# Flamingo-style block on one Trainium2 core: layer 1 of each chunk routed two chunks behind its controllers, and three tables of expert blocks in place of two

## The chip, the cores and the metric

The kernel runs on one core of a Trainium2 chip. The metric is device time of the whole kernel in microseconds (us), one launch, all data in float32 in device memory at the start and at the end. The engines are named as the profile names them: PE (TensorE, the matrix engine), ACT (ScalarE), DVE (VectorE), POOL (GpSimd) and SP (SyncE, which only issues DMAs).

## The reference

2048 tokens (8 batches of 256) of width 128 pass through two layers. The attention of layer 0 has 16 heads of 8; its feed-forward part is a small mixture of 8 experts that is iterated twice. The attention of layer 1 has one head and no projections, and its feed-forward part is a mixture of 8 experts with 512 hidden units.

```python
x = x + tanh(g_xattn[0]) * cross_attention_16_heads(layernorm(x), ctx)
x = x + tanh(g_ffn[0]) * integrator(layernorm(x))
x = x + tanh(g_xattn[1]) * (softmax(layernorm(x) @ ctx.T) @ ctx)
x = x + tanh(g_ffn[1]) * top2_experts(layernorm(x))

def integrator(xf):                       # E=8 experts, top 2, H=64
    w, idx = top2(softmax(gelu(xf @ rw1 + rb1) @ rw2 + rb2))
    v, s = 0, xf
    for _ in range(2):
        c = concat(s, v)
        # one shared controller and two routed ones, each 256 -> 64 -> 3*128
        for (a, b, g) in controllers(c, idx):
            v_next = sigmoid(a) * v - softplus(b) * (s - mu)
            x_next = s + 0.1 * sigmoid(g) * v_next
        halt = sigmoid(gelu(s @ hw1 + hb1) @ hw2 + hb2)
        s, v = s + halt * (mix(x_next) - s), v + halt * (mix(v_next) - v)
    return xf + iw * (gelu(s @ fw1 + fb1) @ fw2 + fb2)      # "refine"

def top2_experts(t):                      # E=8, FF=512
    pr, idx = top_k(t @ Wr + br, 2); w = softmax(pr)
    return sum(w_e * ((silu(t @ W1[e] + b1[e]) * (t @ W2[e] + b2[e])) @ W3[e] + b3[e]))
```

## The kernel before, in words

The tokens are cut into NC = 4 chunks of CH = 512 (two batches, four tiles of 128 each); L = 3 is the last chunk. Every engine has one stream of instructions, written by hand in program order, and the streams meet at semaphores (`wait_ge`, `then_inc`). No scheduler moves anything: an instruction that waits holds up everything behind it on its engine. PE writes into eight banks of PSUM, and most of the waits in PE's stream say that a bank has been read.

**Layer 0.** Attention of all chunks comes first, then the router of the integrator. The integrator runs with the state transposed (width on the partitions). For a chunk, `hidden_unit` (L1885) makes five groups of hidden units: four for pairs of experts and one for the shared controller and the halt gate. ACT takes their gelu; DVE (`mask_first`, L1292) and POOL (L743 and L749) multiply them by the choice masks of the first and of the second expert. Then PE runs the second matrices of the controllers, `controller` (L1944): one matmul from the shared hidden units (L1947), or one for the biases (L1948) and four for the experts (L1950, which fp32 makes eight in the trace). Three of these parts are for softplus (`soft_part`, k = 0 shared, 1 and 2 routed), up to seven for sigmoids (`gate_parts`, L1997: halt, then three `sig_g`, then, in the second pass, three `sig_a`). Softplus is split: DVE adds the bias and caps at 40 (`capped`, L1308), ACT takes Exp and Ln in place (L910), DVE takes the larger of that and the uncapped value (`uncapped`, L1314). `second_step` (L1380) makes the new state.

The first pass (`it` = 0) goes chunk by chunk. The second (`it` = 1) first makes the hidden units of all four chunks, and then goes chunk by chunk through soft parts and gates. Three PSUM banks (5, 6, 7) take turns for the gates.

**Layer 1, attention.** For a chunk c: `refine_up`, two gelus, `refine_down` (the end of layer 0, L2036 to L2060), `add_refined` on DVE, a layer norm whose rstd POOL makes (`rstd_of_chunk`, L653), `second_columns` (transposes, L2062), `second_scores` for batches 2c and 2c+1 (L2075), their maxima on DVE (`maxima2`), exponentials with sums on ACT (`exps2`), `transpose_probs`, `copy_probsT`, `weigh_context`, and `fuse` on DVE.

**Layer 1, routing.** Third layer norm, `rows_to_columns` (L2119), `route_logits` (L2130), `choose` on DVE (top 2 of 8, L1469), `route_ranks` on PE (L2151; small matmuls that count how many tokens of each expert come before), `weights_of` and `slots_of` on DVE, and `send_rows` on POOL (L769): eight indirect DMAs a chunk write the token rows, sorted by expert, to `sorted_x` in device memory. A slot lies in its expert's region of 2048 slots.

In before, this work of chunks 0 and 1 (in part) fills gaps between the gates of chunks 2 and 3; all that remains of chunks 1, 2 and 3 stands in a list behind the last gate, and then come the blocks.

**Layer 1, experts.** BLOCKS = 39 blocks of 128 sorted rows, each of one expert. SP reads a table that DVE made (which expert, where the rows start) and loads for block j the weights (`load_weights`, L594: 516 KB and 256 KB, four buffers) and the rows (`load_rows`, L604, AHEAD = 3 blocks ahead of the weights). The first EARLY = 9 blocks hold only rows of chunks 0 and 1 (`early_blocks`, L1575) and can start before chunks 2 and 3 are routed; the other 30 come from the second table (`late_blocks`, L1587, made by DVE in block 1). A block is `rows_T` (transpose, L2216), `copy_rowsT` on ACT, `up` (eight matmuls, L2226), four silus (L1056), `gated` on DVE (L1655), `down` (L2237), `keep_result` on DVE (L1647) and `send_result` on POOL (L799). The order on PE is:

```python
rows_T(0); rows_T(1)
for j in range(BLOCKS):
    up(j)
    if j + 2 < BLOCKS: rows_T(j + 2)
    if j: down(j - 1)
down(BLOCKS - 1)
```

Behind the last block the results are read back by token and added to x (the tail).

## Time and profile before

| what | value |
|---|---|
| time, median of 3 runs | 647.35 us |
| lowest and highest | 642.56 and 654.7 us |
| the profiled execution | 639.84 us |
| its span in the profile | 638.0 us |
| granted PE clock, mean of it | 0.945 |
| busy over the span: PE, DVE, ACT, POOL | 87%, 67%, 48%, 32% |

All durations come from the one profiled execution. Its span is the time from the first to the last instruction in the record; the time of the execution is 1.84 us longer. PEld, in the rows, is PE's loading of weights, which runs beside the matmuls. A granted clock of 1.00 is 2.4 GHz. A duration of a group of pipelined matmuls is modelled by the profile, so neighbouring groups overlap a little.

### The profile page before, as it was taken

The page shows a single profiled execution, that of the slowest core. Times are in us where ns is not written, and L with a number is a line of the kernel's source. Part 1 is how long each engine was busy: PE and PEld are TensorE (multiplying, and loading weights), DVE is VectorE, ACT ScalarE, POOL GpSimd, SP SyncE. Part 2 cuts the span into 40 slices and gives each one's busy share as a digit, 9 for nine tenths or more (in the row PEclk, how much of TensorE's full clock was granted, in tenths as well). Part 3 has the DMA queues.
Part 4 walks back from the last instruction along what each step waited for, and adds up shares of the span by engine and source line. Part 5 has one row for each costly group of instructions (what it writes and reads, how often), then busy time and mean ns, then how long its engine had stood idle before and what let it go on. Part 6 is the DMA issues. An engine that isn't in the chain of part 4 may idle for free.

```text
span 638.0 us, 9893 instructions
## 1 busy us (share of the span) xinstructions
PE 555.8 (87%) x3294; PEld 329.1 (52%) x3306; DVE 426.1 (67%) x1055; ACT 307.6 (48%) x630; POOL 203.6 (32%) x214
## 2 busy tenths in 40 slices
PE   3876799999998898999999999998764489999991
PEld 1432344443443343444444454455554488999991
DVE  4898889895387899777335766668756174454455
ACT  2653566666658734554353444455341144444440
POOL 4829301011034360004780500012563622333331
PEclk9895999999999998999999999999986789999997
DMA  8685980000079000000040010000016368999975
GB/s 270 150 193 106 175 166 2 3 2 4 1 256 350 25 1 2 0 0 0 1 131 0 2 18 0 2 0 6 29 35 189 107 201 280 332 325 322 324 246 205
DMA packets 48325, 71.18 MB, mean 112 GB/s; under 512 B 11428, under 2 KB 35428, under 8 KB 47988
## 3 DMA queue, kind: packets, MB, share of 16 engines
q1 hardware_dynamic: 45284, 65.61, 35.5%
q0 software_dynamic: 2272, 4.69, 2.0%
q8 instruction: 26, 0.43, 0.3%
q10 hardware_dynamic: 720, 0.27, 0.2%
q14 instruction: 23, 0.19, 0.1%
HBM read 59.18 MB, written 21.29 MB: 126 GB/s over the span
## 4 chain that ended last, share of the span: by engine, by line
PE 65%; DVE 11%; SPq 6%; DMA 6%; ACT 4%; issue 3%; another core or an unknown queue 2%; POOL 2%; POOLq 0%; DVEq 0%
PE psum L1950 18%; PE psum L2226 9%; PE psum L1895 5%; PE psum L2237 5%; PE psum L1752 4%; PE psum L1765 4%; DMA stacks<-maxT 3%; PE psum L1897 3%; PE psum L1773 2%; PE psum L1947 2%; PE psum L1729 2%; DMA stacked<-parts 1%; SPq L513 1%; PE psum L2086 1%
## 5 line engine op out<-in xcount | busy, mean ns | idle before, releaser
L1950 PE MATMUL psum<-hidden,ew 128*128 128x512 f32 x320 | 145.5, 598 | 1.2 <-ACT halt L927 0.6
L856 ACT ACTIVATE probs<-psum 128x512 f32<-128x512 f32 x128 | 74.6, 598 | 50.1 <-PE psum L1752 49.7
L1950 PEld LDWEIGHTS psum<-hidden,ew 128*128 128x128 f32 x320 | 61.3, 192 | 69.8 <-issue 68.5
L1655 DVE SCALAR_TENSOR_TENSOR gated<-psum,wb,silu_g 128x128 f32<-128x128 f32 x156 | 43.9, 344 | 65.1 <-ACT silu_g L1056 57.8
L1136 DVE TENSOR_REDUCE negmax<-psum 128x4 f32<-128x1024 f32 x64 | 76.8, 1210 | 12.5 <-PE psum L1729 11.9
L2226 PE MATMUL psum<-xbT,wb 128*128 128x128 f32 x624 | 79.9, 283 | 1.6 <-DMA wb<-in_wall_dram 1.3
L1056 ACT ACTIVATE silu_g<-psum,wb 128x128 f32<-128x128 f32 x156 | 44.6, 369 | 70.5 <-PE psum L2226 44.9
L2226 PEld LDWEIGHTS psum<-xbT,wb 128*128 128x128 f32 x624 | 75.9, 199 | 2.6 <-DMA wb<-in_wall_dram 1.7
L799 POOL DMA_INDIRECT sorted_y<-yb,xb x39 | 37.6, 964 | 79.0 <-DVE yb L1647 79.0
L1752 PE MATMUL psum<-stacks 50*128 50x256 bf16 x256 | 49.8, 285 | 8.1 <-DMA stacks<-maxT 5.8
L2237 PE MATMUL psum<-wb,gated 128*128 128x128 f32 x312 | 42.3, 279 | 8.9 <-DVE gated L1655 8.5
L749 POOL TENSOR_TENSOR hidden<-unmasked,chosen 128x512 f32<-128x512 f32 x16 | 24.5, 1536 | 63.3 <-ACT unmasked L906 62.3
L1765 PE MATMUL psum<-probs,v_aug 128*32 128x256 f32 x512 | 44.1, 409 | 0.0
L2237 PEld LDWEIGHTS psum<-wb,gated 128*128 128x128 f32 x312 | 38.7, 195 | 9.3 <-issue 9.3
L779 POOL DMA_INDIRECT sorted_x<-xp,slot x32 | 32.0, 999 | 18.7 <-DVE slot L1519 10.1
L1752 PEld LDWEIGHTS psum<-stacks 50*128 50x128 bf16 x256 | 18.6, 97 | 37.4 <-issue 15.8
L1895 PE MATMUL psum<-xT,ew 128*128 128x512 f32 x64 | 32.8, 600 | 1.3 <-ACT routeT L878 1.3
L656 POOL TENSOR_SCALAR rstd<-meanvar 128x4 f32<-128x4 f32 x16 | 3.8, 239 | 92.5 <-DVE meanvar L1074 92.4
L913 ACT ACTIVATE soft<-soft 128x512 f32<-128x512 f32 x24 | 15.1, 627 | 35.7 <-DVE soft L1311 35.6
L1729 PE MATMUL psum<-stacks 48*128 48x256 bf16 x256 | 29.8, 287 | 0.2 <-DVE negmax L1136 0.2
L743 POOL TENSOR_TENSOR hidden<-hidden,chosen 128x512 f32<-128x512 f32 x16 | 22.2, 1418 | 21.9 <-DVE hidden L1300 21.9
L720 POOL COPY v_aug<-xT 128x128 f32<-128x128 f32 x16 | 4.6, 320 | 71.1 <-PE psum L1765 71.0
(255 smaller groups left out, 962.4 us busy)
## 6 DMA issues: line engine op xcount, KB each, us to landing
wb<-in_wall_dram SPq DMA_DIRECT2D x39, 516.0 KB
wb<-in_wall_dram SPq DMA_DIRECT2D x39, 256.0 KB
sorted_x<-in_slots_dram SPq DMA_DIRECT2D x1, 9815.0 KB, 32.3
stacks<-stacked SPq DMA_DIRECT2D x12, 384.0 KB, 8.2
xb<-sorted_x SPq DMA_DIRECT2D x39, 65.0 KB
stacked<-parts SPq DMA_DIRECT2D x6, 384.0 KB, 3.7
back<-sorted_y SPq DMA_DIRECT2D x4, 512.0 KB, 5.2
stacked<-parts SPq DMA_DIRECT2D x6, 256.0 KB, 3.7
```

The lines of the kernel that those rows point to most:

```text
L799: nc.gpsimd.indirect_dma_start(sorted_y, bass.IndirectOffsetOnAxis(ap=home, axis=0), yb[:, j % X_BUFS, :], None).then_inc(yb_out[j % X_BUF ...
L856: nc.scalar.activation(probs[:, g % 2, h % 4, :, :], s2[n % 2].rearrange("p (k q) -> p k q", k=2), ACT.Exp, scale=float(HD) ** -0.5).then_ ...
L1056: nc.scalar.activation(silu_g[:, j % 2, m, :], bank[j % 2][:, m * P:(m + 1) * P], ACT.Silu, bias=wb[:, j % W_BUFS, B1_AT + m:B1_AT + m + 1 ...
L1136: nc.vector.tensor_reduce(negmax[:, p].rearrange("p h q -> p (h q)"), psum[:, i:i + 2, :].rearrange("p h (q k) -> p (h q) k", q=2), AX.X, ...
L1655: nc.vector.scalar_tensor_tensor(gated[:, j % 2, m, :], bank[2 + j % 2][:, m * P:(m + 1) * P], wb[:, j % W_BUFS, B2_AT + m:B2_AT + m + 1], ...
L1729: last = nc.tensor.matmul(bank[s1[n % 2][h]][:, q * S:(q + 1) * S], qs[64 * h:64 * h + ROWS, p, b * S + q * P:b * S + (q + 1) * P], ks[64 ...
L1752: last = nc.tensor.matmul(s2[n % 2][:, k * S:(k + 1) * S], ks[rows, h // 2, b * S + k * P:b * S + (k + 1) * P], qs[rows, h // 2, b * S:(b ...
L1765: last = nc.tensor.matmul(o[b % 2][32 * j:32 * j + 32, (g // 2) * S:(g // 2 + 1) * S], v_aug[:, b % BC, k, 4 * g + j, :], probs[:, g % 2, ...
L1895: last = nc.tensor.matmul(dst, w[:, 0, :], xT[:, chunk(c)], start=True, stop=not it)
L1950: last = nc.tensor.matmul(dst, ew2[:, j, cols], hidden[:, c, k - 1, j, :], start=False, stop=(j == 3))
L2226: last = nc.tensor.matmul(bank[2 * i + j % 2][:, m * P:(m + 1) * P], w[:, i * FF + m * P:i * FF + (m + 1) * P], xbT[:, j % 2, :], start=Tr ...
L2237: last = nc.tensor.matmul(bank[4 + j % 2][:, 0:D], gated[:, j % 2, m, :], w[:, m * D:(m + 1) * D], start=(m == 0), stop=(m == MT - 1))
```

## The change

**1. Softplus.** `capped` goes from DVE. ACT now reads PSUM itself and takes three functions, Abs, Exp (scale -1) and Ln (bias 1), and DVE adds max(value, 0) in one instruction. The biases of the shared controller and of the halt gate become a 97th row of their matrices, against a row of ones that POOL writes once.

**2. Second pass.** It goes chunk by chunk from the hidden units on. Work of layer 1 stands in fixed places of each chunk's turn: the refine, columns and scores of the chunk before it, and the probabilities, rows, logits and ranks of the chunk two before it. Gates use two banks (5 and 6); routing has bank 7 for itself. The order of gates is sig_g of 1, 2, 0, halt, sig_a of 1, 2, 0. `second_step` has fewer instructions, and `choose`, `weights_of`, `slots_of` of chunk c-2 and the first table stand in it.

**3. Blocks.** The tables are EARLY = 9 (chunks 0 and 1), MIDDLE = 8 (with chunk 2) and LATE = 22. Behind the last gate only the attention of chunk 2 and the refine of chunk 3 are left ahead of block 0; the routing of chunk 2, and scores, fusion and routing of chunk 3, stand between blocks 0 and 12 on all engines. SP waits for a table and its rows before block 9 and before block 17. `rows_T` and `down` have one bank each where they had two. The weights of the second expert are a power on POOL for all chunks (in before chunks 1 to 3 took an exponential on ACT). Context for the second attention is loaded chunk by chunk.

The core of the diff (banks, waits that only follow them, and the layout of `chosen` and of the weights left out):

```diff
@@ softplus on ACT @@
 def softplus(it, c, k):
-    act.wait_ge(capped_ready, 3 * (NC * it + c) + k + 1)
+    n = NC * it + c
+    act.wait_ge(soft_psum, 3 * n + k + 1)
+    if n >= 2:
+        act.wait_ge(state_ready, n - 1)
     t = soft[:, k, c % 2, :]
-    steps.then(nc.scalar.activation(t, t, ACT.Exp))
+    steps.then(nc.scalar.activation(t, soft_bank(it, c, k)[:], ACT.Abs))
+    steps.wait()
+    steps.then(nc.scalar.activation(t, t, ACT.Exp, scale=-1.0))
@@ second pass and the first blocks on PE @@
+for c in range(NC):
+    hidden_units(c)                 # refine_up(c - 1) ahead of its fifth unit
+    soft_part(1, c, 0)
+    if c: refine_down(c - 1)
+    if c >= 2: transpose_probs(2 * c - 4)
+    soft_part(1, c, 1)
+    if c >= 2: transpose_probs(2 * c - 3)
+    soft_part(1, c, 2)
+    if c >= 2: weigh_context(2 * c - 4); weigh_context(2 * c - 3)
+    if c: second_columns(c - 1)
+    gate_part(1, c, 0); gate_part(1, c, 1)
+    if c >= 2: rows_to_columns(c - 2)
+    if c: second_scores(2 * c - 2); second_scores(2 * c - 1)
+    gate_part(1, c, 2); gate_part(1, c, 3)
+    if c >= 2: route_logits(c - 2)
+    gate_part(1, c, 4)
+    if c >= 2: route_ranks(c - 2)
+    gate_part(1, c, 5); gate_part(1, c, 6)
+transpose_probs(4); transpose_probs(5)
+weigh_context(4); weigh_context(5)
+refine_up(L); refine_down(L)
...
 up(j)
 if j + 2 < BLOCKS: rows_T(j + 2)
+if j == 1: second_columns(L)
+if j == 2: second_scores(6)
+if j == 3: route_ranks(2)
+if j == 5: transpose_probs(7)
+if j == 7: rows_to_columns(L)
+if j == 9: route_ranks(L)
 if j: down(j - 1)
+if j == 0: rows_to_columns(2)
+if j == 1: route_logits(2)
+if j == 3: second_scores(7)
+if j == 4: transpose_probs(6)
+if j == 5: weigh_context(6); weigh_context(7)
+if j == 7: route_logits(L)
@@ the same blocks on ACT, behind the silus of block j @@
+if j == 1: copy_xT2(L)
+if j == 5: copy_probsT(7)
+if j == 7: copy_xT3(L)
 if j + 2 < BLOCKS: copy_rowsT(j + 2)
+if j == 0: copy_xT3(2); copy_rows(2)
+if j in (2, 3): exps2(j + 4)        # behind a load of the exp table
+if j == 4: copy_probsT(6)
+if j == 7: copy_rows(L)
@@ the same blocks on DVE @@
+if j == 2: maxima2(6)
+if j == 3: slots_of(2)
+if j == 8: choose(L)
+if j == 9: slots_of(L)
 if j: keep_result(j - 1)
-if j == 1: late_blocks()
-if j == 3: expert_shares()
+if j == 1: choose(2)
+if j == 2: weights_of(2)
+if j == 3: maxima2(7)
+if j == 4: table_of_blocks(1, middle_table, MIDDLE, middle_ready)
+if j == 5: sums_of(L); fuse(6); fuse(7); third_stats(L)
+if j == 6: layer_norm_rows(L)
+if j == 9: weights_of(L)
+if j == 11: table_of_blocks(2, late_table, LATE, late_ready)
+if j == 13: expert_shares()
@@ the same blocks on POOL @@
 send_result(j)
+if j == 0: second_weights(2)
+if 2 <= j < 6:
+    if j == 4: rstd_of_chunk(3, L)
+    send_rows(2, range(2 * (j - 2), 2 * (j - 1)))
+if j == 7: second_weights(L)
+if 8 <= j < 12: send_rows(L, range(2 * (j - 8), 2 * (j - 7)))
@@ SP, behind the nine early blocks @@
+sp.wait_ge(middle_ready, 1)
+sp.wait_ge(middle_rows, 16 * GR)
+load_blocks(EARLY, EARLY + MIDDLE)
 sp.wait_ge(late_ready, 1)
-sp.wait_ge(late_rows, 16 * GR * (NC - EARLY_CHUNKS))
+sp.wait_ge(late_rows, 16 * GR)
+load_blocks(EARLY + MIDDLE, BLOCKS)
```

On PE in before, this stands at the end of chunk 3's gates, the last two of which are the pairs L1948 and L1950; L2160 to L2163 are the ranks of chunk 0, whose logits are L2140.

```order
L1948 MATMUL psum<-routeT,eb_rows 128x512
L1950 MATMUL psum<-hidden,ew 128x512 x4
L2072 MATMUL psum<-ident,xn 128x128 x4
L2140 MATMUL psum<-wr,xT 128x8 x4
L1948 MATMUL psum<-routeT,eb_rows 128x512
L1950 MATMUL psum<-hidden,ew 128x512 x4
L2086 MATMUL psum<-chosen,xT 128x256 x4
L2160 MATMUL psum<-is_top,route_b 128x64
L2161 MATMUL psum<-seen,route_b 128x64
```

On PE in the changed kernel, this stands in chunk 2's gates: L2123 are the logits of chunk 0, L1967 and L1969 a gate, L2135 to L2138 the ranks of chunk 0, and L1966 the last gate.

```order
L2123 MATMUL psum<-wr,xT 128x8 x4
L1967 MATMUL psum<-routeT,eb_rows 128x512
L1969 MATMUL psum<-hidden,ew 128x512 x4
L2135 MATMUL psum<-is_top,route_b 128x64
L2136 MATMUL psum<-seen,route_b 128x64
...
L2138 MATMUL psum<-is_top,route_b 128x8
L1967 MATMUL psum<-routeT,eb_rows 128x512
L1969 MATMUL psum<-hidden,ew 128x512 x4
L1966 MATMUL psum<-shared_h,sw 128x512
```

The ranks of chunk 0 moved from behind all gates to a place ahead of two gates of chunk 2, with one gate between them and their logits.

On ACT in before, this is the start of the blocks: the rows of three blocks are copied (L1047) around the silus (L1056), behind one table load.

```order
L1047 COPY xbT<-psum 128x128 x2
L1056 ACT_TABLE_LOAD
L1056 ACTIVATE silu_g<-psum,wb 128x128 x4
L1047 COPY xbT<-psum 128x128
L1056 ACTIVATE silu_g<-psum,wb 128x128 x4
```

On ACT in the changed kernel, this stands in blocks 2 and 3; L1082 are the silus, L1073 the copy, and L1014 the exponentials of batches 6 and 7.

```order
L1082 ACTIVATE silu_g<-psum,wb 128x128 x4
L1073 COPY xbT<-psum 128x128
L1096 ACT_TABLE_LOAD
L1014 ACTIVATE probs,sums<-psum,negmax 128x256 x2
L1082 ACT_TABLE_LOAD
L1082 ACTIVATE silu_g<-psum,wb 128x128 x4
L1073 COPY xbT<-psum 128x128
L1096 ACT_TABLE_LOAD
L1014 ACTIVATE probs,sums<-psum,negmax 128x256 x2
L1082 ACT_TABLE_LOAD
```

Two pairs of exponentials, with a table load ahead of and behind each, moved in between the silus of three blocks.

On POOL in before, the last 16 sends of rows (L779) stand ahead of all sends of results (L799).

```order
L656 TENSOR_SCALAR rstd<-meanvar 128x4
L658 TENSOR_TENSOR rstd<-rstd,minus_half 128x4
L779 DMA sorted_x<-xp,slot 19328x130 x16
L799 DMA sorted_y<-yb,xb 23424x128 x39
```

On POOL in the changed kernel, this stands in blocks 1 to 5; L837 sends a result, L806 rows of chunk 2.

```order
L837 DMA sorted_y<-yb,xb 23424x128 x2
L806 DMA sorted_x<-xp,slot 19328x130 x2
L837 DMA sorted_y<-yb,xb 23424x128
L806 DMA sorted_x<-xp,slot 19328x130 x2
L837 DMA sorted_y<-yb,xb 23424x128
L685 TENSOR_SCALAR rstd<-meanvar 128x4
L687 TENSOR_TENSOR rstd<-rstd,minus_half 128x4
L806 DMA sorted_x<-xp,slot 19328x130 x2
L837 DMA sorted_y<-yb,xb 23424x128
```

The sends of chunk 2 now go two behind each result, and those of chunk 3 likewise behind results 8 to 11.

## Rows read from the trace of the kernel before

**Rows 1.** The span in 40 equal slices: PE busy and granted clock, in tenths.

```profile
PE   3876799999998898999999999998764489999991
PEclk9895999999999998999999999999986789999997
```

**Rows 2.** By stretch: length; busy PE, PEld, DVE, ACT, POOL; clock; DMA share; GB/s.

```profile
324.00:440.00 116.00, 115.10 (x337) 56.51 (x343) 76.33 (x155) 52.66 (x81) 21.76 (x20) 1.00 0.09 21
440.00:498.00 58.00, 37.63 (x220) 30.43 (x219) 39.89 (x195) 21.40 (x50) 31.00 (x35) 0.77 0.28 88
498.00:512.60 14.60, 6.13 (x34) 5.89 (x34) 1.15 (x5) 3.25 (x10) 7.66 (x8) 0.73 0.16 50
512.60:619.80 107.20, 105.44 (x917) 104.65 (x918) 55.52 (x202) 47.51 (x183) 34.82 (x37) 0.98 0.92 302
619.80:638.00 18.20, 4.79 (x60) 3.98 (x59) 9.48 (x18) 2.02 (x8) 2.76 (x3) 0.75 0.52 184
...
511.00:514.70 3.70, 2.06 (x10) 2.09 (x10) 2.25 (x8) 2.40 (x10) 0.00 (x0) 0.50 0.23 61
```

**Rows 3.** The chain of waits, PE in the second pass: start, length, what.

```profile
371.07 1.72 PE psum L2048 x4
...
380.95 1.78 PE psum L2058 x16
...
395.40 0.44 PE psum L2072 x4
...
400.35 1.73 PE psum L2086 x8
...
418.95 1.79 PE psum L2115 x16
...
435.20 0.79 PE psum L2140 x8
```

**Rows 4.** Timeline of PE in the first pass: start, length, group [idle before].

```profile
249.75 0.39 PE L1948 MATMUL psum<-routeT,eb_rows 128*128 128x512 bf16 x1 [2.56 <-ACT halt L927]
249.98 5.29 PE L1950 MATMUL psum<-hidden,ew 128*128 128x512 f32 x8
...
286.03 3.60 PE L1950 MATMUL psum<-hidden,ew 128*128 128x512 f32 x8
```

**Rows 5.** Timeline of DVE: a step of the state, and the choice of experts.

```profile
436.96 0.69 DVE L1421 TENSOR_TENSOR w1t<-w1t,sig_g 128x512 f32<-128x512 f32 x1
...
438.41 0.19 DVE L1474 TENSOR_TENSOR logits<-psum,br 128x32 f32<-128x32 f32 x1
...
440.01 0.22 DVE L1487 TENSOR_TENSOR is_top<-iota,top_atf 128x64 bf16<-128x64 f32 x1
```

**Rows 6.** Timeline of POOL: one send of rows.

```profile
448.03 0.96 POOL L779 DMA_INDIRECT sorted_x<-xp,slot  x1 [0.30 <-issue]
```

**Rows 7.** Timeline of ACT: a table load, an exponential, the first silus.

```profile
440.31 1.28 ACT L1015 ACT_TABLE_LOAD   x1
...
441.61 0.47 ACT L969 ACTIVATE probs<-psum,negmax 128x256 f32<-128x256 f32 x1
...
510.90 1.14 ACT L1056 ACTIVATE silu_g<-psum,wb 128x128 f32<-128x128 f32 x4 [11.28 <-remote]
```

**Rows 8.** Timeline of PE: down of block 0; up steps of two neighbouring blocks.

```profile
512.64 2.05 PE L2237 MATMUL psum<-wb,gated 128*128 128x128 f32 x8 [8.52 <-DVE gated L1655]
...
523.70 1.95 PE L2226 MATMUL psum<-xbT,wb 128*128 128x128 f32 x16
...
526.49 1.95 PE L2226 MATMUL psum<-xbT,wb 128*128 128x128 f32 x16
```

**Rows 9.** Timeline of DVE: first and last step of the first table.

```profile
478.29 0.17 DVE L1549 TENSOR_SCALAR totals<-totals 128x8 f32<-128x8 f32 x1
...
481.06 0.16 DVE L1584 TENSOR_TENSOR used<-taken 128x8 f32<-128x8 f32 x1
```

**Rows 10.** Timeline of SP: the issue of two loads of rows.

```profile
483.98 1.44 SPq L608 DMA_DIRECT2D xb<-sorted_x  x2
```

850 lines of the change are left out of this document (423 added, 427 removed).

## The prediction, made before the changed kernel ran

> **What bounds the kernel now.** Read first the slices of the page: TensorE (PE) is the engine whose row stays at 8 and 9, and its granted clock stays at 9 of 10, except in one hole before the last quarter [rows 1]. The busy time by stretch sizes the hole. From 324 to 440 us, the second pass over the controllers, PE is busy for 115.1 of 116 us. From 440 to 498, the layer-1 work of chunks 1 to 3, it is busy for 37.6 of 58 at a mean clock of 0.77. From 498 to 512.6 it does 6.1 us of work. Then come the blocks, with PE at 105.4 of 107.2 and the DMA engines at 0.92, and a tail of 18.2 us [rows 2]. So the kernel is PE-bound but for 440 to 512.6, where chains through all engines end last: scores, maximum, exponential, transposes, routing, sends, rows. What can be gained lies there: 72.6 us hold only 43.8 us of PE work. The profiled span is 638.0 us and its execution 639.84; the three runs have a median of 647.35, so a profile time has 1.84 added and is multiplied by 1.0117.
>
> **The change part by part.** *First pass.* The cap on the softplus goes, and with it one hop from ScalarE (ACT) to VectorE (DVE). In before, chunk 1's gates wait 2.56 us for a sigmoid, and the eight matmuls behind that wait take 5.29 us where eight usual ones take 3.60 [rows 4]. I count both as gone: 2.56 + 1.69 = 4.3. If the three dependent ACT steps that take the place of the cap are as late, nothing is won: bounds 0 and 4.3. The second pass then starts near 285.5, not 289.6 [rows 4].
>
> *Second pass, added work.* Before needs 150 us to come from 289.6 to 440, nearly all of it PE work. Now it also holds a third refine (1.72 up, 1.78 down), columns of chunk 2 (0.44), scores of four more batches (two take 1.73, so 3.46), transposed probabilities of two (4 transposes each as the columns': 0.9), weighting of two (1.79), rows and logits of chunk 1 (0.44 and 0.79) and two rank steps (some 0.8 each, an estimate: nine matmuls that are narrower than those of the logits) [rows 3]. That is 12.9; 150 becomes 163.
>
> *Second pass, waits.* Each of them is new. A chunk's hidden units now start as soon as the state of the chunk is stepped, and its first soft part waits for the last gelu behind them: about 1 us a chunk, 3 in all, an estimate. The ranks of chunk c-2 stand between gates 4 and 5, and wait for DVE's choice. DVE stands there in a chain of 0.69 us steps, and the choice itself takes from 438.41 past 440.01, some 2 us [rows 5]. Behind the waiting matmul PE's last gates are queued, and behind them ACT's sigmoids and DVE's step. From the logits (gate 4 stands between, 3.6 us of cover) the wait can reach 3.6 us for each of chunks 2 and 3, with up to 1.7 of slow matmuls behind it as in [rows 4]. The rows of chunk 1 wait for a POOL step queued behind eight sends of 0.96 + 0.30 = 1.26 us [rows 6], 10 us in all, most of it under gates: 1.5 is left. Bounds for the whole are 4 and 17 us. The nearest row is the wait of 2.56 us; four like it give 10, which I take. The last gate ends at 285.5 + 163 + 10 = 458.
>
> *From the last gate to the first block.* The last sigmoid (0.6, an estimate from DVE's 0.69 for the same width [rows 5]), a table load (1.28), four exponentials (0.47 each: 1.9), two copies of probabilities (0.6 each, 1.2), weighting 1.79, refine up 1.72, two gelus behind a table load, refine down 1.78 and the first rows. Their order and overlap (the table load of the gelus runs under PE's weighting) make it 13.5 us; bounds 10 and 16 [rows 3, 7]. Here before has 57.8 us (440 to 497.8). The sends of chunks 0 and 1 lie well ahead: 16 x 1.26 = 20 us from a choice near 440. First block at 471.5.
>
> *Blocks.* One takes 526.49 - 523.70 = 2.79 us [rows 8]; 38 of them and the last up step are 107.8. PE's inserts: rows and columns three times 0.44, logits 1.58, two scores 1.73, two transposes 1.0, weighting 1.79, ranks 1.2 makes 8.6. ACT's: twice a table load of 1.28, two exponentials of 0.47 and a load back, 3.5 us each, between silus. A block has some 1.4 us to spare on ACT (four silus of 1.14 together and a copy, against 2.79 [rows 7]), so each stop costs 2.1 or a little more, together 4.5. DVE's: two choices, maxima, places, a fusion, two tables (one takes from 478.29 to 481.06 [rows 9]) and the shares of the experts, near 22 us of small steps, an estimate from [rows 5, 9]. DVE is busy for 55.5 us over the last 38 blocks, 1.46 a block, so 1.3 is to spare in each of 14 blocks [rows 2]: 22 - 18 leaves 4, and their lumps make it 5.7 as seen by PE. Start of the blocks: 2. Boundary to the middle table: POOL puts two sends behind each of results 2 to 5, so a block there costs POOL 3 x 1.26 = 3.8 us against 2.79, and only then may SyncE load three rows (1.44 for two issues, [rows 10]) and the weights: 4. Boundary to the last table: the sends end with result 11, five blocks ahead: 1.5 rather than nothing. Stalls: 2 + 4.5 + 5.7 + 4 + 1.5 = 17.7, less some that overlap, 16; bounds 8 and 25. Then the last up step ends at 471.5 + 107.8 + 8.6 + 16 = 604, where before it is 619.8; the tail of 18.2 stays [rows 2]. Span 622, execution 624, against the runs 624 x 1.0117 = **631 us**.
>
> The row of the table load is the place for a rule. The load takes 1.28 us, and the next activation starts 0.02 us after it ended [rows 7]. The Trainium skill ("ScalarE: Activation LUTs", section "What ACT_TABLE_LOAD costs") puts every switch at a load of 1283 ns and a drain of about 1380 ns, 2.66 us, and speaks against scattering functions of different sets. By the page the four added loads between blocks would cost 10.6 us rather than the 5.1 of the row, and the sum would be some 5 us longer; this trace shows no drain behind the load.
>
> *The hold.* In before ACT's first silu has 11.28 us of idle time ("remote") that no engine of this program explains; PE stands behind it, and it ends soon after the last of POOL's 16 sends [rows 7, 8]. It is put down to nothing that the change keeps, and I don't carry it over. Its bounds are 0 and 11.3.
>
> **The rivals.** *The handovers stall in full.* With every wait at its upper bound (7 in the second pass, 2.5 ahead of the blocks, 9 in them, less the slack they share, 5) the span is 622 + 13.5 = 635.5, 645 against the runs: no change. For it: each handover is a chain through four engines like that of 440 to 498, where PE is idle for 20 us. Against: much less of it is now ahead of PE.
>
> *The hold comes back.* The first silu again stands behind a table load. 631 + 11.4 = 642, no change. For it: an idle time with no visible cause may be bound to that place. Against: by then no sends are under way.
>
> *The clock falls in the blocks: slower than before.* In 511 to 514.7 the granted clock is 0.50, the lower level of 1.2 GHz, behind the hold, and it comes back to 0.98 when PE is dense [rows 2]; down(0) takes 2.05 us there [rows 8]. Now the handover and each insert leave gaps in the first 13 blocks. At the lower level a block takes 2.79 us more, 36 for 13; half a block's room opens for ACT and DVE, so that 14.5 of the stalls are absorbed. Net +22: span 644, 653 against the runs. The point: this beats the 16 us of gain from about 9.5 blocks on (1.67 net a block), and passes +2% from 15 or 16 blocks on. For it: the mean clock of 0.77 in the gappy stretch 440 to 498. Against: between 324 and 440 the same mixture of long matmuls and small ones runs at 1.00, and the first blocks are still some three quarters busy (44.9 us of work in 60.9), against 65% in 440 to 498.
>
> *It doesn't do what it says.* Rows of chunk 2 come too late for the middle blocks, and PE waits at block 9 for the rest of the routing. Each send late by one block moves it 2.8 us; five blocks give 14, the same time as the first rival, with which it is counted.
>
> **How the numbers follow.** Forecast 0.58; its own range is 618 to 645, three quarters of what the bounds of its waits add up to on either side (-17.5 and +18.5). Handovers in full 0.16, hold 0.11, clock 0.15. A measurement of this kernel tells about 2% from no change: under 634.4 is faster, over 660.3 slower. Of the forecast's 0.58 some 0.42 lie under 634.4, the rest within; with 0.03 of the rivals where a stall elsewhere is smaller, faster is 0.45. Of the clock's 0.15 half lies above 660.3, and with 0.05 where two rivals meet slower is 0.13. The rest, 0.42, is no change. The range of 614 to 656 leaves out a tenth on each side.
>
> **What would show it.** Right: the last gate of chunk 3 ends near 458 and the first up step starts near 471; blocks 13 to 38 pass at 2.79 us; the last up step ends near 604, and the tail lasts 18. PE's idle time before the ranks is 2 to 4 us in chunks 2 and 3. A table load between blocks takes 1.28 us with no gap behind it. Wrong: a granted clock under 0.8 anywhere in blocks 0 to 12 (then the clock rival); an idle time over 5 us at block 9 or 17 (the tables); an idle time of ACT above 10 us at the first silu (the hold); a second pass that ends past 465 (then its waits were underrated).

## The result, and the profile after

The changed kernel takes 659.82 us (median of 4 runs, 657.51 to 662.08), the kernel before 644.95 (4 runs, 635.73 to 654.7). The ratio is 1.0323, with a 95% interval of 1.0208 to 1.0439: slower by 3%, where 2.5% faster was forecast. The profiled execution takes 657.51 us with a span of 655.7. Every kernel has some executions with a lower granted clock and a longer time (one of e2's four took 941.91 us at a mean of 0.55), and the ratios leave these out, while the medians of the experiments do not.

The slices of the page answer to [rows 1]. The hole before the last quarter is gone, and in its place there are smaller ones between the 29th slice and the 35th.

```profile
PE   3867799999988899999989999888679667799991
PEclk9785999999999999999999999999879959999996
```

By stretch (columns as in [rows 2]): second pass, from its last gate to the first block, blocks 0 to 7 with the wait for the second table, blocks 8 to 16, blocks 17 to 38, tail.

```profile
290.20:473.40 183.20, 166.22 (x516) 80.96 (x514) 111.09 (x256) 81.35 (x129) 58.12 (x52) 0.99 0.08 17
473.40:489.50 16.10, 10.26 (x47) 7.64 (x47) 7.42 (x21) 7.80 (x16) 6.38 (x7) 0.79 0.38 111
489.50:535.40 45.90, 32.97 (x263) 31.41 (x263) 25.41 (x120) 22.72 (x61) 18.11 (x20) 0.86 0.56 176
535.40:575.00 39.60, 32.09 (x251) 30.99 (x252) 19.89 (x88) 12.60 (x47) 17.71 (x19) 0.91 0.73 222
575.00:637.80 62.80, 60.01 (x531) 59.24 (x530) 29.18 (x106) 27.62 (x107) 20.15 (x21) 1.00 0.91 300
637.80:655.70 17.90, 3.76 (x51) 2.95 (x49) 9.46 (x18) 1.01 (x5) 1.92 (x2) 0.70 0.54 187
```

PE is idle for 17.0 us of the second pass and for 20.4 us of the first 17 blocks, and the handover between them takes 16.1 us where it took 58.

The traces are compared stage by stage from here on, since one stage varies by itself. Attention and router end (the first hidden units start) at 174.0 us in the first trace of the kernel before, at 172.2 and 190.0 in two more (r2 and r1), and at 192.5 and 196.2 in two variants with the same attention (e4 and e11). The window 80 to 100 us shows what goes with it: PE is granted its full clock in one trace and half of it in another, with the same program. The first line is of the kernel before, the second of r1, the same kernel once more.

```profile
80.00:100.00 20.00, 19.46 (x213) 8.64 (x207) 17.43 (x32) 13.36 (x25) 0.53 (x2) 1.00 0.70 127
```

```profile
80.00:100.00 20.00, 20.00 (x124) 7.55 (x128) 10.19 (x14) 7.33 (x14) 0.53 (x2) 0.50 0.80 159
```

So the table counts from the first hidden units. Each number is a difference of starts of matmuls in the trace: first pass, second pass to the end of its last gate, from there to up 0, up 0 to up 38 (38 blocks), and up 38 to the end. It is no output of the profiler.

| kernel | first pass | second pass | to block 0 | 38 blocks | rest | sum |
|---|---|---|---|---|---|---|
| before | 115.5 | 150.2 | 58.1 | 120.9 | 19.3 | 464.0 |
| r1_before | 117.0 | 150.2 | 57.9 | 121.3 | 19.3 | 465.7 |
| r2_before | 115.4 | 150.2 | 57.8 | 123.4 | 21.0 | 467.8 |
| e4_before_no_late_sends | 113.7 | 150.2 | 56.3 | 110.3 | 19.5 | 450.0 |
| changed | 113.0 | 183.2 | 16.1 | 146.2 | 20.0 | 478.5 |
| r3_after | 111.3 | 185.0 | 16.1 | 145.5 | 21.1 | 479.0 |
| e1_ranks_later | 113.0 | 175.4 | 19.2 | 143.1 | 19.8 | 470.5 |
| e2_sends_together | 111.3 | 185.0 | 16.1 | 132.4 | 20.0 | 464.8 |
| e3_no_late_sends | 111.3 | 184.9 | 16.3 | 136.4 | 19.5 | 468.4 |
| e5_boundary | 111.3 | 186.6 | 16.0 | 142.1 | 21.5 | 477.5 |
| e6_listed | 111.3 | 183.2 | 52.6 | 112.9 | 21.9 | 481.9 |
| e7_ranks_sends_boundary | 112.9 | 175.4 | 18.3 | 139.6 | 22.6 | 468.8 |
| e8_ranks_all_sends | 113.0 | 175.3 | 18.5 | 144.2 | 19.7 | 470.7 |
| e9_split_97 | 111.3 | 183.2 | 16.1 | 145.3 | 19.9 | 475.8 |
| e10_split_ranks_sends | 112.8 | 177.0 | 18.6 | 143.4 | 19.6 | 471.4 |
| e11_before_spread | 115.3 | 150.2 | 56.2 | 119.6 | 19.6 | 460.9 |
| e12_before_softplus_spread | 111.3 | 150.0 | 56.4 | 121.4 | 19.3 | 458.4 |
| e13_softplus_97_whole | 111.3 | 150.0 | 58.3 | 121.0 | 19.5 | 460.1 |
| e14_softplus_97_split | 111.3 | 150.0 | 58.2 | 123.3 | 19.3 | 462.1 |
| e15_softplus_two_pieces | 112.9 | 150.0 | 58.1 | 122.4 | 19.5 | 462.9 |

Of the span's 17.7 us, 14.5 lie behind the first hidden units: 2.5 won in the first pass, 33.0 lost in the second, 42.0 won in the handover, 25.3 lost in the blocks, 0.7 lost at the end. The other 3.2 are lost ahead of them.

**Second pass.** The timeline of PE shows the waits in front of the ranks of chunks 0 and 1 (L2135) and, between them, the rows of chunk 1 (L2111):

```profile
414.77 0.20 PE L2135 MATMUL psum<-is_top,route_b 128*128 128x64 bf16 x1 [3.17 <-DVE is_top L1516]
...
454.80 0.66 PE L2111 MATMUL psum<-ident,xp 128*128 128x128 f32 x4 [1.96 <-DVE xp L1130]
...
466.52 0.20 PE L2135 MATMUL psum<-is_top,route_b 128*128 128x64 bf16 x1 [3.17 <-DVE is_top L1516]
...
467.28 5.29 PE L1969 MATMUL psum<-hidden,ew 128*128 128x512 f32 x8
```

The ranks wait 3.17 us both times, and behind the second wait the same 5.29 us stand for eight matmuls as in [rows 4]. Each of the turns of chunks 1 to 3 adds two waits of 0.77 to 1.15 us for a gelu.

**The second table.** PE ends up 7 at 519.6 and then waits 11.4 us, in block 7, not in block 9:

```profile
531.01 0.48 PE L2197 MATMUL psum<-ident,xb 128*128 128x128 f32 x1 [11.40 <-DMA xb<-sorted_x]
```

The chain of waits runs back from there:

```profile
519.65 1.05 POOL rstd L687
...
526.13 2.29 DMA sorted_x<-xp,slot
...
529.22 1.75 DMA xb<-sorted_x
...
531.01 0.48 PE psum L2197
```

L2197 is the transpose of the rows of block 9, which PE's stream has in front of down 6. It needs the last send of chunk 2, which stands behind result 5 and, on POOL, behind the rstd of chunk 3.

### The profile page after: what moved, and what is told of

Same layout as the page of the kernel before. It is cut to its first block, busy times and chain, and to the rows that moved or that the text cites. A ratio compares the mean times of both kernels' runs of the same rounds, so it can differ in the third digit from the quotient of the medians.

```text
span 655.7 us, 9999 instructions
## 1 busy us (share of the span) xinstructions
PE 563.0 (86%) x3307; PEld 329.4 (50%) x3307; DVE 420.3 (64%) x1054; ACT 326.1 (50%) x655; POOL 205.4 (31%) x218
## 4 chain that ended last, share of the span: by engine, by line
PE 52%; DVE 15%; SPq 9%; DMA 8%; issue 7%; ACT 5%; POOL 4%; another core or an unknown queue 0%; DVEq 0%; POOLq 0%; ACTq 0%
PE psum L1969 16%; PE psum L2210 6%; PE psum L1771 4%; PE psum L1784 4%; PE psum L2223 3%; POOL sorted_x L806 3%; SPq L525 2%; PE psum L1914 2%; DVE hidden L1342 2%; PE psum L1792 2%; PE psum L1748 2%; PE psum L1966 2%; DMA wb<-in_wall_dram 2%; DMA stacked<-parts 2%; DMA stacks<-maxT 1%
## 5 line engine op out<-in xcount | busy, mean ns | idle before, releaser
L1969 PE MATMUL psum<-hidden,ew 128*128 128x512 f32 x320 | 145.5, 598 | 0.0
L1969 PEld LDWEIGHTS psum<-hidden,ew 128*128 128x128 f32 x320 | 61.3, 192 | 67.4 <-issue 66.2
L1082 ACT ACTIVATE silu_g<-psum,wb 128x128 f32<-128x128 f32 x156 | 44.7, 370 | 63.6 <-PE psum L2210 49.5
L837 POOL DMA_INDIRECT sorted_y<-yb,xb x39 | 37.7, 967 | 86.3 <-DVE yb L1641 85.2
L781 POOL TENSOR_TENSOR hidden<-unmasked,chosen 128x512 f32<-128x512 f32 x16 | 21.1, 1320 | 105.9 <-ACT unmasked L957 105.9
L1354 DVE SCALAR_TENSOR_TENSOR soft<-psum,soft 128x512 f32<-128x512 f32 x24 | 16.3, 689 | 51.8 <-ACT soft L973 49.9
L1771 PEld LDWEIGHTS psum<-stacks 50*128 50x128 bf16 x256 | 18.5, 97 | 34.5 <-issue 16.2
L806 POOL DMA_INDIRECT sorted_x<-xp,slot x32 | 31.8, 993 | 12.1 <-issue 9.0
L1914 PE MATMUL psum<-xT,ew 128*128 128x512 f32 x64 | 34.2, 623 | 0.0
L984 ACT ACTIVATE sig_g<-psum 128x512 f32<-128x512 f32 x24 | 14.3, 596 | 28.5 <-PE psum L1969 21.5
L2197 PE MATMUL psum<-ident,xb 128*128 128x128 f32 x39 | 11.2, 288 | 18.0 <-DMA xb<-sorted_x 14.4
## 6 DMA issues: line engine op xcount, KB each, us to landing
sorted_x<-in_slots_dram SPq DMA_DIRECT2D x1, 9815.0 KB, 33.3
```

Of the source, the lines that this page charges most:

```text
L806: nc.gpsimd.indirect_dma_start(sorted_x, bass.IndirectOffsetOnAxis(ap=slot[:, 2 * t + k:2 * t + k + 1], axis=0), xp[:, t, k, :], None).the ...
L1082: nc.scalar.activation(silu_g[:, j % 2, m, :], bank[j % 2][:, m * P:(m + 1) * P], ACT.Silu, bias=wb[:, j % W_BUFS, B1_AT + m:B1_AT + m + 1 ...
L1771: last = nc.tensor.matmul(s2[n % 2][:, k * S:(k + 1) * S], ks[rows, h // 2, b * S + k * P:b * S + (k + 1) * P], qs[rows, h // 2, b * S:(b ...
L1914: last = nc.tensor.matmul(dst, w[:, 0, :], xT[:, chunk(c)], start=True, stop=not it)
L1969: last = nc.tensor.matmul(dst, ew2[:, j, cols], hidden[:, c, k - 1, j, :], start=False, stop=(j == 3))
```

## Experiments

The edits are shown shortened: counts of loads, semaphore increments and lines that only follow are left out. Each ratio is against runs of the kernel before that were taken with it. Sizes of single stages come from one trace of each kernel.

### Known waits of the changed kernel: e1, e2, e5, e7, e8

e1, order on PE:

```diff
 gate_part(1, c, 4)
-if c >= 2: route_ranks(c - 2)
 gate_part(1, c, 5)
+if c >= 2: route_ranks(c - 2)
 gate_part(1, c, 6)
```

> The ranks of chunks 0 and 1 stand behind gate 5 rather than gate 4, with two gates between them and their logits; nothing else is changed. Theory (the waits of the second pass are DVE's choice, 3.17 us in front of the ranks in chunks 2 and 3, and the slow matmuls behind one of them): both idle times go to 0, the last gate ends some 6 to 8 us sooner than 473.3, and the span is 6 to 8 us shorter unless the blocks take it back. Rival (DVE is the bound of a turn, since the slots and the table only move later by the gate that was put ahead): the idle time moves to the next chunk's hidden units, and the gates end within 2 us of 473.

Measured: 659.98 us median against 635.4, ratio 1.0354 (1.0249 to 1.0459). The second pass takes 175.4 us, 7.8 less, and the ranks of chunk 1 no longer wait (no idle time at their row in the timeline of PE):

```profile
474.50 0.19 PE L2135 MATMUL psum<-is_top,route_b 128*128 128x64 bf16 x1
```

The theory on the wait holds. But 3.1 of the 7.8 come back ahead of block 0: the sends of chunk 1 are later too, and PE now waits 1.36 and 1.30 us for the first two loads of rows. The time of the whole kernel shows no gain outside its interval.

e2, on POOL (the rstd of chunk 3 stays behind result 4):

```diff
-if 2 <= j < 6: send_rows(2, range(2 * (j - 2), 2 * (j - 1)))
+if j == 2: send_rows(2, range(GR))
```

> The eight sends of chunk 2 go in one piece behind result 2 rather than two behind each of results 2 to 5. Theory (the hole of 12 us in PE at the first row of block 9 is the wait for the last of these sends, which result 5 and the rstd of chunk 3 hold back): the last send starts near 517 rather than 526, and the hole ends 7 to 9 us sooner; the time falls by 5 to 8 us, since results 3 to 5 are sent later. Rival (sends of rows in a piece hold ACT and DVE, as the 11.28 us of the kernel before and gaps of 2.8 to 6.2 us beside sends suggest): ACT and DVE stand still for up to 10 us beside the eight sends, and the time falls by less than 3 us or rises.

Measured: 656.67 us median, ratio 1.0343 (1.0242 to 1.0445). From up 7 to up 8 it takes 7.9 us in place of 17.8, and the 38 blocks take 132.4 in place of 146.2. The last of the eight sends starts at 525.47, 28.5 us behind up 0, where it was 36.6. The transpose of block 9's rows (here still in block 7) waits 2.42 us:

```profile
530.46 0.33 PE L2197 MATMUL psum<-ident,xb 128*128 128x128 f32 x1 [2.42 <-DMA xb<-sorted_x]
```

So the place of the sends (behind results 3 to 5 and the rstd) was most of the hole. The ratio does not show it: against the changed kernel the span of its trace is 6.4 us shorter, and its attention 7.3 us longer, so that the gain stands in this trace alone.

e5, on PE, at j + 1 = 9 and 17:

```diff
 up(j)
-if j + 2 < BLOCKS: rows_T(j + 2)
+if j + 2 < BLOCKS and j + 2 not in FIRSTS and j + 1 not in FIRSTS: rows_T(j + 2)
 if j: down(j - 1)
+if j + 1 in FIRSTS: rows_T(j + 1); rows_T(j + 2)
```

> At blocks 9 and 17 PE transposes the first rows of the new table only after the up and down steps that don't need them (order up 8, down 7, rows 9, rows 10 in place of up 7, rows 9, down 6, up 8, rows 10, down 7). Theory (part of the hole is only order: PE's queue has down 6, the logits of chunk 3, up 8 and down 7 behind the waiting transpose): 6 to 8 us of work move into the hole at block 9 and 2 to 3 at block 17, and the time falls by 6 to 10 us. Rival (the rows set the pace of everything behind them, SP's weights too, and the blocks then end as late as before): the hole keeps its end, and block 9 starts within 2 us of where it did.

Measured: 657.4 us median, ratio 1.0362 (1.0276 to 1.0448). Down 6, the logits, up 8 and down 7 now run in the hole, but up 9 then waits for its weights, which SP issues behind three loads of rows:

```profile
534.91 0.33 PE L2197 MATMUL psum<-ident,xb 128*128 128x128 f32 x1 [3.88 <-DMA xb<-sorted_x]
...
540.06 3.78 PE L2210 MATMUL psum<-xbT,wb 128*128 128x128 f32 x16 [3.65 <-DMA wb<-in_wall_dram]
```

From up 7 to up 10 it takes 24.6 us in place of 26.3. The rival holds: PE's order was not the price, the rows' way through POOL and SP was.

> All three edits (ranks a gate later, chunk 2's sends in a piece, rows of the new table behind the work that doesn't need them). Theory (three separate waits): the gains add up to 15 to 22 us, and the kernel lands near 640, at or under the kernel before. Rival (they are in one chain and share it): no more than the largest of the single gains, under 10 us.

Measured: 656.34 us, ratio 1.0447 (1.0364 to 1.053). The second pass keeps its 7.8, the blocks take 139.6, more than in e2 alone. From up 7 to up 11, where the third edit acts, it takes 25.5 us (17.5 in e2), so it probably costs more than it saves once the sends are early; the ranks are later here too, so that this is not shown apart. e8 has the first two edits and the sends of chunk 3 in a piece:

```diff
-if 8 <= j < 12: send_rows(L, range(2 * (j - 8), 2 * (j - 7)))
+if j == 8: send_rows(L, range(GR))
```

> The ranks a gate later, and both chunks' eight sends in one piece each (behind results 2 and 8). From the single runs: the second pass is 7.8 us shorter, of which 3 come back ahead of block 0; the hole at block 8 is 10 us shorter; the late table's wait (up to 8 us at block 16) should fall by some 4. Theory (these three waits are apart): 460 - 4 = 456 us from the first hidden units to the end, against 478.5 of the changed kernel and 464 of the kernel before. Rival (the sends in a piece hold the engines beside them, so what the first piece gave the second takes): over 462 us.

Measured: 660.1 us, ratio 1.0243 (1.0115 to 1.0371); 470.7 us from the first hidden units, not 456. The rival holds. The second piece has its price as well: block 12 to 13 takes 11.6 us. Beside the first piece ACT stands for 8.68 us with a cause that is none of the program's engines, and PE behind it; the timeline of ACT:

```profile
526.00 0.59 ACT L1022 COPY probsT<-psum 128x512 f32<-128x512 f32 x1 [8.68 <-remote]
```

### The hold beside sends: e3, e4, e11, r1, r2, r3

In e3 the sends of chunk 3 are left out of the changed kernel, in e4 the 16 of chunks 2 and 3 out of the kernel before, each with the wait for them.

> The eight sends of rows of chunk 3 and the wait for them are left out, so that the output of chunk 3 is made of other rows (its results are read from chunk 0's). Theory (sends in a piece hold ACT and DVE): the idle times of ACT (4.72) and DVE (6.22) near block 12 and those of 2.42 and 1.78 near block 15 go, and blocks 10 to 16 pass at 2.8 us each: some 8 us less. Rival (the holds come from the weights' DMAs or from the engines' instructions): they stay where they are, and only the wait at the late table (2.4 us) goes.

> The kernel before, with its 16 sends of rows of chunks 2 and 3 left out (the output of these chunks is made of the rows of chunks 0 and 1). Theory (the hold of 11.28 us in front of the first silu comes from the 16 sends in a piece): it goes, and the span is 10 to 14 us shorter than 638. Rival (the hold is ACT's own, behind the load of the silu table): 11 us stay.

> The kernel before, once more, for its trace. Theory (the hold of 11.28 us at the first silu belongs to the 16 sends in a piece): it is there again, 8 to 14 us between blocks 0 and 1 beyond the usual gap. Rival (a hold comes now and then, in any kernel): it is absent or elsewhere. The attention stage (up to the first hidden units, 174.0 us in the first profile) should differ from run to run by up to 18 us if the clock of PE sets it.

> As the run before it, a third trace of the kernel before: if the hold is systematic it is in all three, and the stretch from the first hidden units to the end is 464 us within 3; if it is sporadic, some of them have 453.

> The changed kernel once more, for its trace. From the first hidden units to the end it had 478.5 us, with one hold of 4.2 us at block 12. Theory (the two waits are its order, the hold comes now and then): the hole at block 8 (17.8 us from up 7 to up 8) and the two waits of 3.17 us in front of the ranks are there again, the hold at block 12 is not: 474 us. Rival (the hold belongs to the sends of chunk 3): it is there again.

Measured, one trace each (times 655.87, 644.54, 657.54, 641.81 and 661.82 us). From the start of up 0 to that of up 2 (the expectations call it up 0 to up 1) it takes 16.7, 16.0 and 16.5 us in the three traces of the kernel before, and 6.7 in e4; two usual blocks take 5.6. The first silu of the kernel before, in r1 and then in e4:

```profile
527.22 1.14 ACT L1056 ACTIVATE silu_g<-psum,wb 128x128 f32<-128x128 f32 x4 [10.41 <-remote]
```

```profile
514.76 1.14 ACT L1054 ACTIVATE silu_g<-psum,wb 128x128 f32<-128x128 f32 x4 [0.71 <-PE psum L2224]
```

So the hold at the first silu is systematic in the kernel before, and it goes with the sends.

In the changed kernel the place is free of it (8.0 and 7.7 us from up 0 to up 2), but block 12 to 13 takes 7.0 and 7.8 us in its two traces, beside the sends of chunk 3:

```profile
553.95 1.12 DVE L1649 SCALAR_TENSOR_TENSOR gated<-psum,wb,silu_g 128x128 f32<-128x128 f32 x4 [6.22 <-remote]
```

Without these sends, in e3, it takes 2.8 us. That alone does not tie the two together, since e1, e2, e5 and e7 keep these sends as they are and pass block 12 in 2.8 us too. What the sends cost for certain is the wait for the third table: from up 12 to up 17 it takes 14.9 us in e3, 21.4 and 21.9 in e1 and e2, and 23.7 in the changed kernel, where the stop at block 12 comes on top.

In e11, a variant of the kernel before, the sends stay, in two lots:

```diff
-for c in range(EARLY_CHUNKS, NC): send_rows(c, range(GR))
+send_rows(2, range(GR))
 ...
 send_result(j)
+if j < 4: send_rows(L, range(2 * j, 2 * j + 2))
```

> The kernel before, with the eight sends of chunk 3 taken out of the piece of 16 and put two behind each of results 0 to 3. Up 0 to up 1 took 16.7, 16.0 and 16.5 us in three traces of the kernel before and 6.7 without the 16 sends. Theory (an engine that waits beside a long piece of sends is let go only when it ends): the gap falls to 6 to 9 us, the second table's rows are there in time for block 9, and the time falls by 6 to 10 us. Rival (the first silu's hold is bound to the place, not to the length of the piece): the gap stays at 16.

Measured: ratio 0.9932 (0.9867 to 0.9997), medians 649.95 and 648.51. Up 0 to up 2 takes 6.1 us, and the first silu waits 0.32:

```profile
519.95 1.15 ACT L1057 ACTIVATE silu_g<-psum,wb 128x128 f32<-128x128 f32 x4 [0.32 <-PE psum L2227]
```

The hold is gone with the long piece, but up 7 to up 8 takes 9.0 us, as the second table's rows are late now. Of 10 us some 3 to 7 stay (461 us from the first hidden units, against 464.0 to 467.8). What in a piece of sends holds another engine is open: in e2, e7, e8 and e10 the same piece of eight follows result 2, and only e8 and e10 have the hold. In e1 POOL issues 14 indirect DMAs one behind another from 552.4 us on, and no engine has an idle time of this kind beside them.

### The parts of the change: e6, e12, e10

e6 undoes the third part: every insert of the block loop stands ahead of it, on all engines.

```diff
 refine_down(L)
+rows_to_columns(2); second_columns(L); route_logits(2); second_scores(6); route_ranks(2); second_scores(7)
+transpose_probs(6); transpose_probs(7); weigh_context(6); weigh_context(7)
+rows_to_columns(L); route_logits(L); route_ranks(L)
```

> The changed kernel with its third part undone: all the routing of chunk 2 and all of chunk 3's layer 1 stand in a list ahead of block 0, tables and softplus and second pass as changed. It prices the third part against the second. By my sum the list costs PE some 33 us between the last gate and block 0 in place of 16, and the blocks then take 108 us in place of 149. Theory (hiding the routing between blocks cost more than it hid): this runs 10 to 20 us faster than the changed kernel, near 640. Rival (the second pass with its stalls is what lost): the time stays near 655 to 660.

Measured: 665.16 us, ratio 1.0594 (1.0503 to 1.0685). The rival holds, and more: the list takes 52.6 us (36.5 more than the changed kernel's handover), the blocks 112.9. By stretch: second pass, list, blocks.

```profile
291.70:474.90 183.20, 166.24 (x516) 81.00 (x514) 110.18 (x251) 81.35 (x129) 57.02 (x50) 0.99 0.07 17
474.90:527.50 52.60, 28.00 (x128) 21.60 (x127) 26.32 (x129) 15.20 (x32) 19.34 (x22) 0.63 0.28 88
527.50:640.40 112.90, 109.30 (x943) 108.12 (x943) 56.63 (x208) 51.20 (x191) 43.17 (x45) 0.98 0.89 292
```

Against this run, the third part wins 36.5 us ahead of the blocks and gives 33.3 back in them. Against the kernel before, the second part costs 33.0 us in the second pass and takes only 5.5 off the list. A list of half the routing is hardly shorter: PE is busy for 28.0 of its 52.6 us, as it was for 37.6 of 58 [rows 2]. So its length is not PE's work; that it is the chain of the last chunk is my reading, which no run tests. (The list is mine, not that of the kernel before, and uses fewer banks; a better one might be shorter.)

e12 is e11 with the first part of the change alone, the matrices of 97 rows loaded as 96 rows and 1.

> As the run before, and with the change's first part (the softplus without the cap and the biases as a 97th row, loaded as 96 rows and 1), but neither its second pass nor its third table. By the forecast the first pass gains 0 to 4.3 us, and the changed kernel's traces have 111.3 to 113.0 us for it where the kernel before has 115.4 to 117. Theory (the first part is a gain of its own): 2 to 4 us less than the run without it, in the first pass. Rival (ACT's third function makes the softplus of the second pass late): no gain, and PE waits in the second pass.

Measured: 640.39 us against 648.51, ratio 0.9904 (0.9862 to 0.9946): 1% ahead of the kernel before, and the lowest ratio of the study, though those of e11 and e15 (below) are within its interval. First pass 111.3 us against 115.3 in e11, second pass 150.0 against 150.2. First and second pass:

```profile
185.90:297.20 111.30, 105.13 (x312) 46.09 (x312) 87.01 (x216) 72.94 (x115) 31.16 (x24) 1.00 0.28 91
297.20:447.20 150.00, 149.69 (x422) 71.02 (x421) 84.81 (x163) 73.49 (x113) 45.21 (x35) 1.00 0.07 16
```

> The split load, the ranks a gate later and chunk 2's sends in a piece. By the single traces: 478.5 - 4.8 (second pass and handover) - 10 (hole) = 464 us from the first hidden units, that start at 173: 637 us of span, and as fast as the kernel before within 1%. Rival (what one gives the next wait takes, as in the run with the three edits): 645 or more.

Measured: ratio 1.0037 (0.9982 to 1.0092), so no change against the kernel before, as expected by the theory. The ratio rests on three of its ten runs (643.87, 644.46 and 649.25 us); the median of all ten is 660.66. The one trace is of a run of 658.62 us and does not bear the theory's sum out: it shows the hold of e8 (8.71 us) and 471.4 us from the first hidden units, not 464. By the ratio the load, the ranks and the sends together are worth about the loss that was measured; stage by stage it is not shown.

### The start: e9, e13, e14, e15

In each trace of a kernel that loads 97 rows whole, SP stands at the two DMA issues behind the load of `sw2`. In the first trace of the changed kernel the first stacked keys (L545) are issued at 28.38. The timeline of SP:

```profile
12.86 4.11 SPq L525 DMA_DIRECT2D hw<-in_hw_dram  x1
17.01 4.40 SPq L525 DMA_DIRECT2D mu<-in_mu_dram  x1
...
28.38 1.43 SPq L545 DMA_DIRECT2D stacked<-parts  x3
```

In the kernel before the same three are:

```profile
13.41 0.43 SPq L513 DMA_DIRECT2D hw<-in_hw_dram  x1
13.88 0.43 SPq L513 DMA_DIRECT2D mu<-in_mu_dram  x1
...
21.17 1.45 SPq L533 DMA_DIRECT2D stacked<-parts  x3
```

While SP stands at the second of the two issues, the DMA engines do next to nothing. The window 18 to 20 us, first in the changed kernel and then in the kernel before (the last two columns are DMA share and GB/s; a packet counts whole in the window in which it starts, so a share can pass 1):

```profile
18.00:20.00 2.00, 2.00 (x6) 1.31 (x6) 1.18 (x9) 0.59 (x1) 1.68 (x3) 0.50 0.07 25
```

```profile
18.00:20.00 2.00, 2.00 (x4) 0.73 (x3) 1.34 (x12) 1.12 (x3) 1.52 (x3) 0.50 1.11 192
```

e9 loads the two matrices in two pieces each, behind the other matrices:

```diff
-(sb1, "sb1"), (sw2, "sw2"), (hw2, "hw2"),
+(sb1, "sb1"),
+for dst, src in ((sw2, "sw2"), (hw2, "hw2")):
+    sp.dma_start(dst[0:96, :], a[src][0:96, :])
+    sp.dma_start(dst[96:HROWS, :], a[src][96:HROWS, :])
```

> The changed kernel with each of the two matrices of 97 rows loaded as 96 rows and 1 row. In every trace of the changed kernel and its variants SP stands 3.7 to 4.6 us and then 4.4 us at the two DMA issues behind the first of these loads, where it took 0.43 each in the kernel before, and the first loads of the stacked keys come 7 us later. Theory (a load of 97 rows is what holds SP): both issues take 0.4 to 0.5 us again, the stacked keys are issued near 22 us instead of 28, and the first hidden units start near 173 us instead of 177 to 181: 4 to 8 us less. Rival (the fewer loads in front only moved a wait for queue space that is there anyway): the issues wait as long somewhere else.

Measured: ratio 1.0229 (1.0173 to 1.0286), where the changed kernel has 1.0323 (1.0208 to 1.0439) in its own comparison, so the two are not told apart. The issues wait no longer, and the stacked keys come at 21.33:

```profile
16.32 0.32 SPq L527 DMA_DIRECT2D hw<-in_hw_dram  x1
16.68 0.28 SPq L528 DMA_DIRECT2D hw<-in_hw_dram  x1
...
21.33 1.46 SPq L548 DMA_DIRECT2D stacked<-parts  x3
```

Its hidden units start at 185.1 all the same, with PE at half its clock from 80 to 100 us, so the trace does not settle what the wait costs. Three kernels run on one chip come closer. e13 is e12 with whole loads, e14 is e12 again, and e15 sends chunk 3's rows as four behind result 0 and four behind result 1.

> The run e12 again, with the two matrices of 97 rows loaded whole, as the changed kernel does. Theory (the whole load costs the start of the attention stage what SP waits): SP waits 3.7 to 4.6 and 4.4 us at the next two issues, and the time is 4 to 8 us above the run with the split loads on the same chip. Rival (the attention stage absorbs it, as the trace of e9 left open): SP waits, and the two times agree within 2 us.

> The run e12 unchanged, as the partner of the run above on the same chip. It should again be 0.5 to 1.4% faster than the kernel before (0.9904 in e12), by 4 us of the first pass and what is left of the hold.

> As the run above, with chunk 3's eight sends as four behind result 0 and four behind result 1. In e12 up 7 to up 8 took 9.2 us, as the last sends came behind result 3. Theory (the second table's rows are late by the pacing): the sends end some 5 us sooner, that gap falls to 3 to 5 us, and the time is 4 to 6 us below the run above. Rival (a longer piece holds the engines again): another gap of 5 to 10 us opens beside the pieces, and the time does not fall.

Measured: whole 1.0053 (0.9973 to 1.0133), lowest time 642.02; split, lowest times 636.03 (e14, for which there is no ratio) and 635.94 (e15, ratio 0.9937, 0.9877 to 0.9996). The lowest times differ by 6 us and the ratios by 1.2%, some 7 us. The two intervals overlap a little; that of e12, the kernel of e14 on another chip, does not overlap with that of e13. SP in e13:

```profile
12.93 4.23 SPq L511 DMA_DIRECT2D hw<-in_hw_dram  x1
17.20 4.40 SPq L511 DMA_DIRECT2D mu<-in_mu_dram  x1
```

So by the times the whole loads of 97 rows cost some 6 to 7 us, a cost that stands in no term of the forecast. The traces do not show all of it: the hidden units start at 180.6 us in e13 and at 178.7 in e14.

e15 is not faster than e14, and here the theory and its rival both came true. Up 7 to up 8 takes 2.8 us in place of 10.4, so the rows of the second table were late by the pacing. But up 4 to up 5 takes 12.2 us, beside ten indirect DMAs of POOL in a row (a result, four sends, a result and four sends), with ACT at a stand for 10.01 us:

```profile
532.85 1.14 ACT L1066 ACTIVATE silu_g<-psum,wb 128x128 f32<-128x128 f32 x4 [10.01 <-remote]
```

## Why the prediction was wrong

The profiled span is 33.1 us longer than the sum of the terms (622.6 before it was rounded): 15.9 in the blocks up to the end of the last up step, 10.2 in the second pass, 4.7 ahead of it and 2.6 in the handover, while the tail is 0.3 shorter.

**Cap of the softplus: right.** Forecast 4.3 us less in the first pass. The changed kernel has 2.5 less in its first trace (3.4 us of it at half the clock) and 4.2 in the second; e12 against e11 has 4.0.

**Loads of the first part: missed.** The sum has no term for the row of ones and the longer matrices. What they changed is the load: the DMA of 97 rows. In the traces the two issues behind it take 8.5 us in place of 0.9, and by the times of e13 to e15 it costs 6 to 7 us. The Trainium skill has a rule that bears on it ("DMA: Bandwidth & Descriptors", section "Why a DMA increments its semaphore by 16 and not by 1"): the number of DMA engines is the largest up to 16 that divides the slowest dimension, so that 96 rows get 16 and a prime like 97 gets one. The trace agrees: from 18 to 20 us the DMA share is 0.07, about one engine of 16, where it is 1.11 in the kernel before and 0.77 in e9 with the loads split at 96. Why SP stands meanwhile neither of them says.

**Work in the second pass: about right.** Forecast 12.9 us more; e1, with the clock at 1.00 throughout, has 164.4 us of PE work against some 149.7 in the pass of e12, 14.7 more.

**Waits in the second pass: undersized.** Forecast 10, bounds 4 and 17. Measured 17.0 of idle time and 1.7 of slow matmuls, 18.7 in all. I had the places and the upper bounds of the single waits (3.6 for the ranks; 3.17 measured, twice) and then took four waits like the nearest row. The trace has 13. For the ranks the bound was nearly the value.

**Last gate to block 0: right in its mechanism.** Forecast 13.5, measured 16.1, 0.1 past its bound. The stretch has a mean granted clock of 0.79, and the weighting and refine up take 3.78 and 2.57 us in place of the 1.79 and 1.72 that the sum had from rows at the full clock: 2.8 us more, the whole difference.

**Blocks: the step that failed.** Forecast 16 us of stalls, bounds 8 and 25; measured 146.2 - 106.0 for 38 blocks at 2.79 - 8.6 of inserts (the forecast's own sum) = 31.6. The term "boundary to the middle table: 4" is the mis-sized one. Up 7 to up 8 took 17.8 us, 15.0 more than a block. I had priced POOL's pace, but two things stand beside it. The last sends wait for result 5 and for the rstd of chunk 3, 36.6 us behind up 0. And PE meets the wait two blocks sooner, at `rows_T(9)` in block 7, so the cover of blocks 7 and 8 was not there. e2 takes 9.9 of the 15.0 away by moving the sends ahead of results 3 to 5 and of the rstd. e5 shows that PE's order by itself is worth only 1.7. The boundary to the last table was mis-sized in the same way: 1.5 in the sum, and 8.8 from up 12 to up 17 (23.7 against 14.9 in e3), some 2 of it the stop at block 12. For the start of the blocks and the lumps of ACT and DVE, 12.2 in the sum, some 8 are left, so these were not too low.

**The hold: left out rightly at its place, for want of a cause.** I left the 11.28 us of the kernel before out as tied to nothing that the change keeps. It is tied to POOL's sends (16.7, 16.0, 16.5 us from up 0 to up 2; 6.7 without them, 6.1 with them apart), and at the first silu of the changed kernel, with no sends beside it, it is gone, so the rival that it comes back there did not come true. The changed kernel has a stop of the same look at block 12, 4.2 and 5.0 us beyond 2.8, of which some 2 reach the end of the stretch; with the same sends e1, e2, e5 and e7 have none, so its condition is open.

**The rivals.** The nearest was the first, all handovers stalled in full, at 645: its mechanism came true and its price was too low: the middle boundary alone went 11.0 us past its term, where the rival had 9 more for all waits of the blocks. The last rival, counted with it, named the very place: PE waits for the rows of chunk 2 at the middle table, at a price of 14 us. It was right, at 15.0 us. The clock rival did not come true, though its sign did (under 0.8 anywhere in blocks 0 to 12): the granted clock is 0.50 for 17.1 us from 522.2 on, of which 8.8 are the idle end of the hole, and for 3.4 us from 556.3 on, behind the stop at block 12. Elsewhere in the first 17 blocks it is 1.00, so it fell behind the waits and was not their cause, and the 10 blocks that the rival needed are far off.

**The trade as a whole.** The forecast took 44 us off the handover and paid 23 in the second pass and 10 in the blocks. The first number came true (42.0). The prices were 33.0 and 25.3, more than it even without the load.

## What to carry to other kernels

Work that is moved out of a stretch in which the engine waits into one in which it is full costs its full time, while the stretch it left shrinks only if the work was on its chain: half the routing gone made the list 5.5 us shorter (with the list of e6) and the full stretch 33 us longer. At the start of a new table or buffer, look in the engine's own order for the first instruction that touches it, prefetches too, and count the cover from there; but find out first what the data itself waits for, since that was most of the hole here. And a change that adds one row to a tile changes its DMA: 97 rows in one load were slow here, and 96 and 1 were not.
